# The last expert stage of an eight-sequence tower, reordered as a pipeline over batches

## The reference

```python
flat = hidden_states.reshape(b * s, h)                 # 4096 x 256, layer norm of h
probs = softmax(flat @ router_w + router_bias)         # 16 experts
top_w, top_i = top_k(probs, 2)
norm_w = top_w / (sum(top_w) + 1e-6)
combine = sum(one_hot(top_i, 16) * norm_w[..., None], axis=1)
routed = combine[:, 15:16] * flat                      # expert 15 is the identity
for e in range(15):
    y = silu(flat @ gate_w[e]) * (flat @ up_w[e]) @ down_w[e]   # width 128
    routed = routed + combine[:, e:e + 1] * y
gate = conv1d(x_ncw, conv_w, window 3, causal)         # shared expert
shared = silu(gate) * (hidden_states @ shared_up_w) @ shared_down_w
return h + shared + routed
```

## Time and profile before

| | us |
|---|---|
| median of three runs | 2643.86 |
| the profiled execution | 2641.9 |
| its span, first to last instruction | 2640.2 |
| mean granted TensorE clock | 0.907 of full speed |
| PE busy | 2182.8 (83%) |
| DVE busy | 1586.9 (60%) |
| ACT busy | 1325.2 (50%) |
| POOL busy | 744.7 (28%) |

### The profile page before, as it was taken

How to read it: one execution, slowest core, us unless ns; L and a number is a source line. 1 busy time by engine, 2 the same in 40 slices (tenths; PEclk the granted TensorE clock), 3 DMA queues, 4 the chain that set the end, 5 groups by cost and what they waited for, 6 DMA issues and landing times. The chain is left out here.

```text
span 2640.2 us, 43175 instructions
## 1 busy us (share of the span) xinstructions
PE 2182.8 (83%) x13073; PEld 1686.4 (64%) x13073; DVE 1586.9 (60%) x4474; ACT 1325.2 (50%) x2652; POOL 744.7 (28%) x835
## 2 busy tenths in 40 slices
PE   3899999999999999767882873888888989695982
PEld 2788888887888888635662651555555556463772
DVE  4555665565556656356764977767777768541225
ACT  2344544454445444345545763867776768210330
POOL 5111111111111111042446662122212222226442
PEclk8899999999999999989986985988989989678996
DMA  5620010000000000022232535222122221303446
GB/s 108 166 33 0 11 33 1 8 13 24 1 8 3 1 1 0 27 65 51 43 64 68 147 109 177 78 67 64 49 70 74 71 69 51 101 33 108 127 137 243
DMA packets 209472, 165.36 MB, mean 63 GB/s; under 512 B 108320, under 2 KB 167376, under 8 KB 209296
## 3 DMA queue, kind: packets, MB, share of 16 engines
q1 hardware_dynamic: 190832, 120.71, 17.3%
q0 software_dynamic: 14240, 38.35, 4.6%
q10 hardware_dynamic: 4224, 4.19, 0.5%
HBM read 91.07 MB, written 72.11 MB: 62 GB/s over the span
## 5 line engine op out<-in xcount | busy, mean ns | idle before, releaser
L630 PE MATMUL psum_o<-w_s,hid_s 128*128 128x256 f32 x3072 | 384.0, 284 | 19.1 <-ACT hid L434 19.1
L616 PE MATMUL psum_h<-xn2T_s,w_s 128*128 128x512 f32 x1536 | 389.9, 404 | 5.4 <-ACT hid L434 3.6
L630 PEld LDWEIGHTS psum_o<-w_s,hid_s 128*128 128x128 f32 x3072 | 371.8, 188 | 27.0 <-issue 19.1
L433 ACT ACTIVATE hid_s<-psum_h,b 128x512 fp32r<-128x512 f32 x256 | 176.5, 689 | 391.5 <-PE psum_h L616 376.0
L616 PEld LDWEIGHTS psum_h<-xn2T_s,w_s 128*128 128x128 f32 x1536 | 283.5, 191 | 87.1 <-ACT hid L434 21.8
L2126 DVE CUSTOM_DVE_ANT_0 ra_z<-ra_psum_s,rhat 128x128 f32<-128x128 f32 (+3 forms) x512 | 224.9, 483 | 132.6 <-PE ra_psum_s L2234 120.5
L2076 ACT ACTIVATE ra_z<-ra_z,ra_nm 128x128 f32<-128x128 f32 (+3 forms) x512 | 245.4, 563 | 0.0
L2007 POOL TENSOR_SCALAR_AFFINE_SELECT ra_z<-ra_z 128x512 f32<-128x512 f32 x128 | 81.6, 637 | 477.3 <-DVE ra_z L2157 477.3
L2246 PE MATMUL ra_psum_p<-ident,ra_z 128*128 128x128 f32 x1280 | 181.4, 293 | 1.3 <-ACT turned L2068 1.3
L517 DVE TENSOR_TENSOR hid_s<-hid,hid_s 128x1024 fp32r<-128x1024 f32 x128 | 156.0, 1223 | 43.1 <-ACT hid L434 42.1
L2068 ACT ACTIVATE turned<-ra_psum_p 128x1024 f32<-128x1024 f32 x128 | 131.3, 1026 | 92.1 <-PE ra_psum_p L2246 92.1
(11 more groups left out here) (380 smaller groups left out, 4212.4 us busy)
## 6 DMA issues: line engine op xcount, KB each, us to landing
ex_slots<-blank SPq DMA_DIRECT2D x1, 10296.0 KB, 33.8
ex_zT<-ex_slots SPq DMA_DIRECT2D x39, 264.0 KB, 3.0
ex_rows<-ex_slots SPq DMA_DIRECT2D x8, 1056.0 KB, 9.3
w<-in_L_tok_w SPq DMA_DIRECT2D x8, 1024.0 KB, 7.5
ra_scratch<-ra_hi SPq DMA_DIRECT2D x32, 256.0 KB
ra_scratch<-ra_lo SPq DMA_DIRECT2D x32, 256.0 KB
ra_q_st<-ra_scratch SPq DMA_DIRECT2D x128, 64.0 KB, 1.8
ra_k_st<-ra_scratch SPq DMA_DIRECT2D x128, 64.0 KB, 1.8
```

The source lines that it names most:

```text
L433: act.activation(hid_s[:, 0, m, :], psum_h[:, m % 2, :], ACT.Gelu, bias=b1[:, m:m + 1])
L616: mm = pe.matmul(psum_h[:, m % 2, :], w1_s[:, w_part, k, m * P:(m + 1) * P], xn2T_s[:, x_part, k, :], start=(n == 0 and k == 0), stop=(n = ...
L630: mm = pe.matmul(psum_o[:, t // 2, (t % 2) * D:(t % 2 + 1) * D], hid_s[:, h_part, m, t * P:(t + 1) * P], w2_s[:, w_part, m, :], start=(n = ...
```

## The change

The stage does the same computation with another order and another layout of `ex_slots`.

- Each of the 15 experts has a region of 4096 + 128 rows of its own. So a token's row is known as soon as its own batch and those before it are counted. 78 dummy blocks lie behind the regions; the early clearing now covers these alone, with the same number of rows as before. The end of each expert's last block is made blank at the end of the front: 15 stores of a tile `pads` (8 by SP, 7 by ACT), each at a row read into a register.
- The front runs in steps, one for each batch. DVE does `settle(i-1)` (slot numbers), `norm_stats(i+2)`, `hidden(i-1)`, `norm_apply(i+2)`, `add_shared(i-2)`, `choose(i)`. `choose` uses the operations for the eight greatest values and their places in the stead of reductions and comparisons. POOL does `rstd_of(b+2)` and then `scatter(b)`: four stores of the first choice, a fill of the result places in a second buffer `rows1`, four stores of the second choice. ACT copies the rows of a batch to `rows1`. PE does `turn(b)`, `shared_gate(b-1)`, `count(b-1)`, `shared_up(b-1)`, `shared_down(b-2)`, `router(b)`.
- The statistics of batches 0 and 1 come ahead of the preparation of the convolution weights.
- `table()`, at the end, works out for each of the 78 blocks its owner and its first row in `ex_slots`. The softmax parts (`soft`, `shares`) come after it.
- In the pair loop the two blocks of a pair no longer lie side by side: SP reads a row number into a register and issues a load for each block. `RING` grows from 6 to 10, `YRING` from 4 to 8.

The core of the diff:

```diff
-            for c in range(2):
-                sp.wait_ge(sent[c], 16 * NT)
+            sp.wait_ge(pads_made, 2)
+            sp.wait_ge(pad_ready, 1)
+            for e in range(0, EX, 2):
+                at = sp.value_load(pad_at[0:1, e:e + 1], min_val=0, max_val=DUMMY - P)
+                sp.dma_start(slots[ds(at, P), :], pads[:, e, :]).then_inc(pad_stored, 16)
+            sp.wait_ge(S.ex_cleared, 16)
+            sp.wait_ge(table_ready, 2)
             sp.wait_ge(gu_done, NB)
+            sp.wait_ge(pad_stored, 16 * EX)
+            sp.wait_ge(sent, 16 * NT)
+            for n in range(2):
+                sp.wait_ge(sent1[n], 8 * NT)
             for j in range(PAIRS):
                 if j >= RING:
                     done, value = sent_before(j - RING)
                     sp.wait_ge(done, value)
-                sp.dma_start(zs[:, j % RING, :, :], slots[2 * j * P:(2 * j + 2) * P, :]...).then_inc(zs_loaded[j % RING], 16)
+                for s in range(2):
+                    at = sp.value_load(row_at[0:1, 2 * j + s:2 * j + s + 1], min_val=0, max_val=DUMMY + (BLOCKS - 1) * P)
+                    sp.dma_start(zs[:, j % RING, s, :], slots[ds(at, P), :]).then_inc(zs_loaded[j % RING], 16)
...
+            def scatter(b):                                  # POOL
+                pool.wait_ge(slot_ready, b + 1)
+                for n in range(b * TT, (b + 1) * TT):
+                    pool.indirect_dma_start(slots, bass.IndirectOffsetOnAxis(ap=slot[:, 0, n:n + 1], axis=0),
+                                            rows[:, n, :], None).then_inc(sent, 16)
+                if b >= 2:
+                    pool.wait_ge(sent1[b % 2], 16 * TT * (b // 2))
+                pool.iota(rows1[:, b % 2, :, D].bitcast(I32), ...).then_inc(marked, 1)
+                pool.wait_ge(marked, b + 1)
+                pool.wait_ge(copied, b + 1)
+                for t in range(TT):
+                    pool.indirect_dma_start(slots, ..., rows1[:, b % 2, t, :], None).then_inc(sent1[b % 2], 16)
...
+            for b in range(NB):
+                if b + 2 < NB:
+                    rstd_of(b + 2)
+                scatter(b)
...
+            norm_stats(0)                                    # DVE
+            norm_apply(0)
+            norm_stats(1)
+            prepare()
+            norm_apply(1)
+            for i in range(NB):
+                if i >= 1:
+                    settle(i - 1)
+                if i + 2 < NB:
+                    norm_stats(i + 2)
+                if i >= 1:
+                    hidden(i - 1)
+                if i + 2 < NB:
+                    norm_apply(i + 2)
+                if i >= 2:
+                    add_shared(i - 2)
+                choose(i)
+            add_shared(NB - 2)
+            settle(NB - 1)
+            table()
+            soft()
+            hidden(NB - 1)
+            shares()
+            add_shared(NB - 1)
...
+            turn(0)                                          # PE
+            prepare()
+            router(0)
+            for b in range(1, NB):
+                turn(b)
+                shared_gate(b - 1)
+                count(b - 1)
+                shared_up(b - 1)
+                if b >= 2:
+                    shared_down(b - 2)
+                router(b)
+            shared_down(NB - 2)
+            count(NB - 1)
+            shared_gate(NB - 1)
+            shared_up(NB - 1)
+            shared_down(NB - 1)
...
-        RING, YRING = 6, 4
+        RING, YRING = 10, 8
```

More of the change, by code:

```diff
@@ L2293, in experts_stage @@
     DOWN = 2 * DK * I
-    NEVER = -3.0e38
     with ExitStack() as ctx:
@@ L2305, in experts_stage @@
         w = sb("w", [P, EX * WROW])
-        rows = sb("rows", [P, NT, ROWLEN])
+        rows, rows1 = sb("rows", [P, NT, ROWLEN]), sb("rows1", [P, 2, TT, ROWLEN])
         zT = sb("zT", [P, DK, NB * TP])
@@ L2309, in experts_stage @@
         var_eps, rstd = sb("var_eps", [P, NT]), sb("rstd", [P, NT])
[L2310 to L2315, removed]
+        gate, hid = sb("gate", [I, T]), sb("hid", [I, 2, T])
@@ L2516, in norm_apply @@
                 last.then_inc(z_ready, 1)
[L2518 to L2528, removed]
@@ new lines, in soft, with shares @@
+            def soft():
+                dve.tensor_tensor(other[:, :, :], logits[:, :, :], best[:, 0, :].unsqueeze(2).to_broadcast([P, NT, E]), ALU.subtract).then_inc(soft_in, 1)
+                dve.tensor_tensor(gap[:, :], best[:, 0, :], best[:, 1, :], ALU.subtract).then_inc(soft_in, 1)
+            def shares():
+                dve.wait_ge(soft_out, 1)
+                link(dve.tensor_reduce(total[:, :], other[:, :, :], AX_X, ALU.add))
+                link(dve.tensor_scalar(den[:, :], total[:, :], 1e-6, 1.0, ALU.mult, ALU.add))
+                link(dve.tensor_tensor(den[:, :], den[:, :], second[:, :], ALU.add))
+                link(dve.reciprocal(share[:, 0, :], den[:, :]))
+                link(dve.tensor_tensor(share[:, 1, :], share[:, 0, :], second[:, :], ALU.mult))
@@ L2665, in router, with count @@
                                        start=(k == 0), stop=(k == DK - 1))
                 mm.then_inc(logits_done, 1)
-            turn(0)
-            pe.wait_ge(prep_copied, 1)
-            for b in range(NB):
-                if b + 1 < NB:
-                    turn(b + 1)
-                router(b)
-            def shared_first(b):
+            def count(b):
+                if b == 0:
+                    pe.wait_ge(consts_made, 2)
+                else:
+                    pe.wait_ge(counts_taken, b)
+                pe.wait_ge(chosen_ready, b + 1)
+                each = bank[7][:, 0:2 * TT * E].rearrange("p (w e t) -> p w e t", w=2, e=E)
+                by_expert = chosen[:, :, :].rearrange("p t e -> p e t")
+                pe.matmul(each[:, 0, :, :], ones[:, :], by_expert, start=True, stop=True)
+                pe.matmul(each[:, 1, :, :], below[:, :], by_expert, start=True, stop=True).then_inc(counted, 1)
```

296 lines of the change are left out of this document (161 added, 135 removed).

## The result

The changed kernel took 2620.23 us (median of 4 runs, 2617.73 to 2623.75) against 2646.93 for the kernel before in the same rounds: ratio 0.9899, 95% interval 0.9883 to 0.9915. That is 26.7 us less; 16.1 us were predicted. The profiled execution took 2620.42 us, with a span of 2618.7.

The account below looks back on a forecast made before the run. Bounds: a serial front of norms, routing and 64 stores, then a pair loop held by its six-buffer ring. Loop -23.6, loop start +1.5 and +1.5, front +4.5 sum to -16.1: 2643.9 to 2627.8, say 2628 us; range 2610 to 2650.

Parts of the forecast that it names:

- Loop, pair 4 to 38: Pair loop: ten buffers end the ring's wait, steps fall from 3.93 to PE's 3.25 us, a gain of 23.6 us.
- Last landing of the front: End of the front: the last indirect store lands at 2443.3 instead of 2438.83, +4.5 us.
- Landing to pair 4: Start of the pair loop: register read and second load +1.5 us, PE needing pair 1 first +1.5 us.
- The serial turn: Front, batches 0 to 5: stores, power, apply, choose and settle run in series, 19.4 us a turn, 18.1 the first.
- Contention of the stores: Front: stores average 1.02 us instead of 0.96, plus one longer hold-up beside the table, +4 us.
- Batch 5 to 6: Late front, no norm ahead: PE's own work from count to count sets the step, 17.5 us (12 to 23).
- PE's need of 19 us: Front: PE with both slow stretches in each turn needs about 19 us, just under 19.4, so hidden.
- Rival 1: Front: PE stays at its slow level and the turn is 23.0 us; +21, 2649 us; chance 0.12.
- What was to hide: End of front: table (some 8.5 us), blank-row stores (9 to 10 us) and last shared work covered by stores and loads.
- 2: Front: turns not serial and PE not slow, turn 13 us set by POOL and PE; 2590 us; chance 0.08.
- 3: Front: DVE working beside every store holds up POOL's issue; over 0.3% slower from 1.7 us a store; chance 0.05.
- rival 4: Pair loop: another wait takes the ring's place and steps stay at 3.93 us; 2651 us; chance 0.05.

Follow-up runs that it names:

- ring alone: Kernel before with only RING 6 to 10 and YRING 4 to 8, one load a pair, old front: 2624.20 us, ratio 0.992.
- the power between the stores: Changed kernel with the power of batch b+3 queued on POOL between first-choice and second-choice stores of batch b, DVE's order untouched: 2592.34 us, ratio 0.9784.
- powers ahead: Changed kernel with statistics on DVE and power on POOL one batch further ahead: 2583.53 us, ratio 0.977; repeated, 2583.76 us, 0.9766.
- six buffers: Changed kernel with RING back at 6, YRING still 8: 2668.01 us, ratio 1.0088.
- seven buffers: Changed kernel with RING at 7 instead of 10, YRING still 8: 2625.77 us, ratio 0.9917.
- registers read ahead: Changed kernel with RING 6, SP reading both registers of a pair before waiting for the store that frees the buffer: 2646.31 us, ratio 0.9994.

## Why the prediction was right, and where its terms were off

| Term | Predicted | Measured, on the stage's own clock |
|---|---|---|
| Loop, pair 4 to 38 | -23.6 | 110.06 - 133.74 = -23.7 |
| Last landing of the front | +4.5 | 158.1 - 162.2 = -4.1 |
| Landing to pair 4 | +3.0 | 19.6 - 17.7 = +1.9 |
| Sum | -16.1 | -25.9 |

The time was within the range, but the terms didn't all hold. The loop gave what was predicted; the front and its handover to the loop were to cost 4.5 + 3.0 = 7.5 us and gained 4.1 - 1.9 = 2.2, the other sign. These 9.7 us are the whole gap between 16.1 and 25.8. The forecast's own spread of 8 us, 2620 to 2636, only just reaches the 2620.23 measured, and the range down to 2610 had room for the miss; that part of being right is luck.

**The loop** was right, its mechanism and its size. The ring was the cause (ring alone: the same 110.06 us), PE was next at 3.25, and SP's two issues a pair stayed under it.

**The serial turn** was right in kind: the power behind the stores, the apply behind the power, choose behind the apply. The experiment with the power between the stores predicts its own turn to 0.05 us from this reading. DVE's part of one turn, in the changed kernel:

```profile
2336.99 1.38 DVE L2562 TENSOR_SCALAR ex_rows<-x,ex_mv,ex_rstd 128x256 f32<-128x256 f32 x4 [8.80 <-POOL ex_rstd L2431]
2338.29 1.28 DVE L2656 TENSOR_TENSOR x<-ex_bank,x 128x512 f32<-128x512 f32 x2
2339.49 0.21 DVE L2582 TENSOR_TENSOR ex_logits<-ex_bank,ex_rb 128x64 f32<-128x64 f32 x1
...
2342.28 0.29 DVE L2602 TENSOR_TENSOR_SCAN ex_upto<-ex_carry,ex_bank 128x64 f32<-128x64 f32 x1 [0.56 <-PE ex_bank L2754]
...
2344.28 0.17 DVE L2613 CAST ex_slot<-ex_slot_f 128x8 int32<-128x8 f32 x1
```

From the logits to the scan 2.8 us (2.5 taken), from the scan to the end of the cast 2.2 (2.1), from there to the first store 0.3 (0.5), the eight stores 10.1 (10.5). Together 18.9 instead of 19.4, and 17.7 instead of 18.1 for the first.

**The front's end** is the step that failed, 8.6 us in all. On the clock of the kernel before it landed at 2438.99 - 4.3 = 2434.7, not at 2443.3. The parts:
- Contention of the stores, taken at +4 from the earlier trace rows. In the trace only two of 64 stores are clearly longer, 2.06 and 1.21 us beside the table, and the first of a batch 1.04. That is part of the measured turns and of the last batch, which took 10.3 us from first to last store where 9.4 was taken (+0.9). The term of 4 was counted on top and wasn't there. The mean of 1.02 us in the earlier trace rows came from a few long stores, not from all a little (47 of those 64 took at most 1.00 us), and I had spread it over the serial part.
- Batch 5 to 6: 14.3 us instead of 17.5, -3.2. It is PE's own turn, as predicted, from the count at 2398.54 to the next at 2412.84, but 14.3 us long.
- The turns: -0.4 and 4 x -0.5. The first store: +0.5. Batch 6 to 7: -0.3.

The sum, -4 + 0.9 - 3.2 - 2.4 + 0.5 - 0.3 = -8.5, closes the gap.

**Batch 5 to 6 and PE's need of 19 us.** Both rest on the clock. I had both slow stretches of the earlier trace rows in each turn: count, up and down, and then transposes, router and part of the gate. The timeline of PE in one turn of the changed kernel, and two stretches of it (length, busy, clock, DMA share, GB/s):

```profile
2341.86 0.27 PE L2753 MATMUL ex_bank<-ex_chosen,ex_ones 128*128 128x64 bf16 x1 [5.87 <-DVE ex_chosen L2597]
...
2342.06 3.69 PE L2768 MATMUL ex_bank<-ex_zT,ex_s_up 128*128 128x512 f32 x4
2345.55 2.35 PE L2776 MATMUL ex_bank<-ex_s_down,ex_hid 128*128 128x256 f32 x8
2347.74 1.85 PE L2741 MATMUL ex_bank<-ex_rw,ex_zT 128*128 128x16 f32 x16
2349.44 1.07 PE L2730 MATMUL ex_bank<-ident,ex_rows 128*128 128x128 f32 x8
2350.35 5.32 PE L2763 MATMUL ex_bank<-ex_zT,ex_conv_T 128*128 128x512 f32 x12
```
```profile
2342.00:2345.00 3.00, 3.00 (x6) 0.50 0.00 0
...
2350.00:2356.00 6.00, 5.66 (x17) 1.00 0.31 113
```

Up comes behind a pause of 5.9 us and runs at the 1.2 GHz level (3.69 us; 1.90 with powers ahead, where there is no pause). Down speeds up, and router, transposes and gate then run fast: PE is busy 13.8 of 18.9 us in this turn and 14.6 in the next, not 19. The 5.0 us for transposes and router, taken from the slow stretch in the earlier trace rows, were 2.9. Rival 1 was thus further away than "just under": the fall came in each turn, but the slow time lay in the first 3 to 6 us. The Trainium skill (TensorE: Matmul & The Clock Gate, HAM oscillation) says that waits between bursts throw the clock back each time; by that, the trace agrees, with 0.50 to 0.60 in the first 3 us behind each of the five pauses (4.3 to 7.0 us long). What it would have cost was in my sum too high, since the engine was back at 1.00 within the same turn.

**The start of the loop**, +3.0 predicted, was +1.9. The four loads of pairs 0 and 1 go out 1.1 us apart, the first 0.8 behind the landing, and the last lands in 2.2 us, at 2445.35. So the matmuls of pair 0 start 7.3 us behind the last landing of the front (2446.30), against 4.8 before (2443.65), and 0.6 us of these 2.5 come back, as they take 3.17 us instead of 3.73.

**What was to hide, hid.** The table took 8.3 us (2423.95 to 2432.23). The prediction's terms for it, 4 us and four operations that grow from 0.5 to 1.36, give 7.4 and not its 8.5. The eight blank stores of SP began at 2425.40 and took 9.0 us, those of ACT 9.4, the last shared sum ended at 2441.7, and PE began pair 0 at 2443.2. With powers ahead this cover is gone: the last silu behind ACT's blank stores then sets the start of the loop.

**The rivals.** 2: the turns were serial; but the run with powers ahead, 2583.5 us, is close to the time that this rival would have had (2590), with a turn of 11.3 where it had 13. 3: no; with powers ahead DVE was at work beside 56 of the 64 stores, and they took 0.98 us on average. 4: no wait took the ring's place, since ten buffers leave room; with six, the two loads, the register reads behind the wait and the clock that fell with them cost 4.63 - 3.93 = 0.7 us a step, so that rival 4's kind of wait is real and ten buffers are what keeps it away.

## What to carry to other kernels

When a loop is turned into a pipeline, follow each queue past the instruction that was moved: one power of 1 us, queued behind eight stores that belong to another batch, took back nearly all that the front could have given, and moving it alone gave some 28 us more. For a ring of buffers add up the round trip from issue to landing, register reads and second issues included, and divide it by the buffers less the depth of the pipeline; if that is over the step of the busiest engine, add buffers or take work out from behind the wait, and don't count on more once it is under. Try the two-number edit of a large change alone before crediting the rest: here it gave 23 of the stage's 26 us.

## What the runs showed of the hardware

- With six buffers and PE waits of up to 3.2 us the clock was 0.83 to 0.96 in the pair loop; with waits of at most 1.4 us (before), 1.6 (seven buffers) and 1.7 (registers read ahead) it was 1.00. A late load then costs more than its lateness: 1.5 us more on the eight matmuls behind it in the round shown, and nothing behind three of the eleven waits.
- Work that had kept PE at the 1.2 GHz level when it came first (transposes and 16-column matmuls, 0.52 in the earlier trace rows) ran at 1.00 when it came behind up and down in the same turn: 1.85 us for the router, 1.07 for the transposes.
- A register read on SP behind a wait costs 0.7 us before the DMA goes out; read ahead of the wait, the DMA goes out 0.2 us after the landing, and the second 0.5 us behind the first instead of 1.2.
- 62 of the 64 indirect stores of after took 0.95 to 1.09 us, but only 28 of the 64 had DVE at work beside them for more than 0.1 us; with powers ahead 56 had, and the mean was 0.98. The Trainium skill (GPSIMD Engine Reference, Specifications) has the SBUF interfaces shared with VectorE and contended by instructions with two SBUF inputs; by that, the trace agrees for the two that ran beside the table's operations with two inputs (2.06 and 1.21 us; 0.96 beside its reductions), and shows no more of it. With powers ahead one store beside such operations took 1.55 us and another (2387.82) only 0.96.
